# A graph network on one core: the loop over the groups written out, and the light steps at other places among the gate steps

## The reference, cut to what matters

```python
x = _layernorm(x + _L0_gnn_ref(x, adj, W, a_src, a_dst))           # attention, 4 heads: softmax(mask(leaky(...))) @ (x @ W), elu
x = _layernorm(x + _L1_gnn_ref(x, adj, weight, w_ih, w_hh, ...))   # three rounds of: aggregate neighbours, then a GRU cell
x = _layernorm(x + _L2_gnn_ref(x, adj, weight, bias))              # one masked product per relation 1 to 4
x = _layernorm(x + _L3_gnn_ref(x, adj, W, a))                      # attention, 1 head
```

```python
aggr = A.T @ (h @ weight[i])
r = sigmoid(i_r + h_r); z = sigmoid(i_z + h_z); n = tanh(i_n + r * h_n)   # i_* from aggr @ w_ih.T, h_* from h @ w_hh.T
h = (1 - z) * n + z * h
```

## Time and profile before

| what | value |
|---|---|
| median of 3 executions | 3003.52 us (2995.94 to 3004.15) |
| the profiled execution, its own time | 3002.93 us |
| its span, first to last instruction | 3000.9 us |
| mean granted TensorE clock | 0.949 |
| PE busy | 2747.6 us |
| DVE, ACT, POOL busy | 2144.0, 1648.6, 1295.3 us |

### The profile page before, as it was taken

One profiled execution on the slowest core, in us unless ns is written; L12 is line 12 of the kernel. 1 busy time (PEld: TensorE's weight loads), 2 busy tenths in 40 slices (PEclk: granted clock), 3 DMA queues, 4 the chain that ended last, 5 costly groups with the idle time before them and its releaser, 6 DMA issues. The chain is left out here.

```text
span 3000.9 us, 52085 instructions
## 1 busy us (share of the span) xinstructions
PE 2747.6 (92%) x15577; PEld 2353.3 (78%) x15577; DVE 2144.0 (71%) x5170; ACT 1648.6 (55%) x4164; POOL 1295.3 (43%) x1351
## 2 busy tenths in 40 slices
...
DMA packets 97354, 76.18 MB, mean 25 GB/s; under 512 B 6624, under 2 KB 92768, under 8 KB 96992
## 3 DMA queue, kind: packets, MB, share of 16 engines
...
...
## 5 line engine op out<-in xcount | busy, mean ns | idle before, releaser
L943 PE MATMUL psum<-ht_h,whh_h 128*128 128x512 f32 x1152 | 483.5, 420 | 0.0
L943 PE MATMUL psum<-ag_h,wc_h 128*128 128x512 f32 x1152 | 482.4, 419 | 0.0
L943 PE MATMUL psum<-ag_l,wc_h 128*128 128x512 f32 x1152 | 461.6, 401 | 0.0
L943 PE MATMUL psum<-ht_l,whh_h 128*128 128x512 f32 x1152 | 461.4, 401 | 0.0
L943 PE MATMUL psum<-ht_h,whh_l 128*128 128x512 f32 x1152 | 460.1, 399 | 0.0
L943 PE MATMUL psum<-ag_h,wc_l 128*128 128x512 f32 x1152 | 458.4, 398 | 0.0
L1413 POOL TENSOR_TENSOR ht<-ht,g_n 128x512 f32<-128x512 f32 x192 | 256.6, 1336 | 453.9 <-ACT g_n L1104 453.9
L1359 POOL TENSOR_SCALAR rstd<-moments 128x2 f32<-128x2 f32 x256 | 86.6, 338 | 802.1 <-DVE moments L1196 800.6
L943 PEld LDWEIGHTS psum<-ht_h,whh_l 128*128 128x128 f32 x1152 | 220.5, 191 | 54.5
L943 PEld LDWEIGHTS psum<-ag_h,wc_l 128*128 128x128 f32 x1152 | 219.6, 191 | 53.7
L943 PEld LDWEIGHTS psum<-ht_h,whh_h 128*128 128x128 f32 x1152 | 221.8, 193 | 41.6
...
## 6 DMA issues: line engine op xcount, KB each, us to landing
adj_i<-in_adj_dram SPq DMA_DIRECT2D x128, 128.0 KB, 2.1
...
ih_raw<-in_L_gnn_w_ih_dram SPq DMA_DIRECT2D x1, 768.0 KB, 11.9
...
wrs<-in_L_gnn_weight_dram SPq DMA_DIRECT2D x1, 768.0 KB, 11.9
```

What stands on the lines that cost most here:

```text
L943: last = mm(dst, s, m, start=(first and k == 0), stop=(last_part and k == len(flat) - 1))
```

## The change

The loop's segment (groups 2 to 14) becomes 13 segments of one group each, so that all 16 trips are straight code with constants in their waits and addresses. The parts of the program that served the hardware loop go: the second wait in take, the loop in walk, the register forms in after and graphs. TRIP is replaced by another order of the same 254 steps. The order of the gate steps on PE is kept; the light steps, and the shares of gru_n, gru_new, gru_split, gru_turn, gru_turn0, gru_nodes0, gru_keep, gru_norm, gru_load and gru_fin, stand elsewhere. The diff below has the head, some lines of the middle and the tail of TRIP, old and new, and all of the rest.

```diff
 TRIP = """
-last.post_load(0)
-gru_agg(0,0,0)  last.rel_split(0)  next.att_xt(pre,0)
...
-gru_hn(0,0,0)
-gru_rzh(0,0,0)  last.rel_adjt(0)  last.rel_mask(0)  next.att_wh(pre,0,0)  last.gru_fin(1,0)  gru_nodes0(1)
-gru_r(0,0,0)  next.pre_load(0)  last.rel_h1(0)  last.gru_norm(1,0)
-gru_z(0,0,0)  last.gru_fin(1,1)  next.att_wh(pre,0,1)  last.rel_y1(0)  gru_keep(1)
-gru_in(0,0,0)
-gru_hn(0,0,1)  last.rel_rest(0)  gru_load(1)  gru_n(0,0,0)  gru_turn0(1,0)
-gru_rzh(0,0,1)  next.att_scores(pre,0,0)  gru_turn0(1,1)  last.post_load(1)  next.att_scores(pre,0,1)
-gru_r(0,0,1)  last.rel_norm(0)
...
-gru_in(1,1,0)  last.att_res(post,1)  last.rel_rest(2)  gru_turn(0,1,0)
-gru_hn(1,1,1)  gru_turn(0,1,1)  gru_n(1,1,0)  last.att_norm(post,1)
...
-gru_in(1,1,1)  last.att_xt(post,2)
...
-gru_rzh(0,2,1)  gru_split(1,1)  next.att_res(pre,2)  next.pre_load(3)  gru_turn(1,1,0)  last.rel_h1(3)  last.att_pt(post,2,0)
-        gru_turn(1,1,1)  next.gru_load(0)
...
-gru_z(0,2,1)  last.att_pv(post,2)  next.att_wh(pre,3,0)  gru_new(0,2,0)  next.att_norm(pre,2)
-gru_in(0,2,1)  last.rel_y1(3)  last.att_exp(post,2)  last.att_res(post,2)  gru_n(0,2,1)  next.att_wh(pre,3,1)
-        next.att_scores(pre,3,0)  last.rel_rest(3)  next.att_scores(pre,3,1)  gru_new(0,2,1)
-gru_agg(1,2,0)
-gru_agg(1,2,1)  next.att_prob(pre,3)
-gru_hn(1,2,0)  last.att_norm(post,2)
-gru_rzh(1,2,0)  next.att_pt(pre,3,0)  gru_fin(0,0)  next.att_pt(pre,3,1)  next.gru_nodes0(0)  last.rel_norm(3)
-        last.att_store(post,2)
-gru_r(1,2,0)
-gru_z(1,2,0)  last.att_xt(post,3)
-gru_in(1,2,0)  gru_norm(0,0)  gru_fin(0,1)  last.att_wh(post,3,0)  last.att_wh(post,3,1)  next.att_pv(pre,3)
-        last.att_scores(post,3,0)  next.att_exp(pre,3)  last.att_prob(post,3)
-gru_hn(1,2,1)  last.att_pt(post,3,0)  next.att_res(pre,3)  gru_n(1,2,0)  next.gru_keep(0)  next.gru_turn0(0,0)
-        last.att_pv(post,3)  next.gru_turn0(0,1)
-gru_rzh(1,2,1)  next.att_norm(pre,3)  last.att_exp(post,3)
-gru_r(1,2,1)  last.att_res(post,3)
-gru_z(1,2,1)  gru_new(1,2,0)  gru_n(1,2,1)  gru_norm(0,1)
-gru_in(1,2,1)  last.att_norm(post,3)  gru_new(1,2,1)  last.att_store(post,3)
...
+gru_agg(1,1,1)  gru_new(0,1,1)  next.att_exp(pre,1)  gru_split(0,1)
...
+gru_rzh(1,1,0)  last.post_load(3)  last.att_prob(post,1)  last.rel_h1(2)  last.att_pt(post,1,0)
+gru_r(1,1,0)  last.att_pv(post,1)  last.rel_y1(2)  last.att_exp(post,1)  last.att_res(post,1)  next.att_res(pre,1)
...
+gru_in(1,1,1)  next.pre_load(2)  next.att_scores(pre,2,0)
+gru_agg(0,2,0)  gru_n(1,1,1)  next.gru_load(0)
+gru_agg(0,2,1)  next.att_scores(pre,2,1)  last.att_wh(post,2,0)  next.pre_load(3)
+gru_hn(0,2,0)  last.rel_split(3)  next.att_prob(pre,2)
...
+gru_r(0,2,0)  gru_new(1,1,1)  last.att_wh(post,2,1)  next.att_pt(pre,2,0)
...
+gru_rzh(0,2,1)  last.rel_mask(3)  last.att_prob(post,2)  gru_turn(1,1,0)
+gru_r(0,2,1)  next.att_res(pre,2)  last.rel_h1(3)
...
+gru_in(0,2,1)  next.att_wh(pre,3,0)  next.att_norm(pre,2)  last.att_pv(post,2)  gru_n(0,2,1)  gru_turn(1,1,1)  last.rel_y1(3)
+        last.att_exp(post,2)  last.att_res(post,2)  next.att_wh(pre,3,1)  next.att_scores(pre,3,0)
+gru_agg(1,2,0)  last.rel_rest(3)  next.att_scores(pre,3,1)  gru_new(0,2,1)
+gru_agg(1,2,1)
+gru_hn(1,2,0)  last.att_norm(post,2)  next.att_prob(pre,3)
+gru_rzh(1,2,0)  last.rel_norm(3)  next.att_pt(pre,3,0)  gru_fin(0,0)  last.att_store(post,2)
+gru_r(1,2,0)  next.att_pt(pre,3,1)  last.att_xt(post,3)  next.gru_nodes0(0)
+gru_z(1,2,0)  gru_norm(0,0)  gru_fin(0,1)  last.att_wh(post,3,0)  last.att_wh(post,3,1)  last.att_scores(post,3,0)
+        next.att_pv(pre,3)  next.gru_keep(0)  last.att_prob(post,3)  next.att_exp(pre,3)
+gru_in(1,2,0)  next.att_res(pre,3)  last.att_pt(post,3,0)  next.gru_turn0(0,0)  next.gru_turn0(0,1)  gru_n(1,2,0)
+        last.att_pv(post,3)  gru_new(1,2,0)
+gru_hn(1,2,1)
+gru_rzh(1,2,1)  last.att_exp(post,3)  gru_norm(0,1)  last.att_res(post,3)
+gru_r(1,2,1)
+gru_z(1,2,1)  gru_n(1,2,1)
+gru_in(1,2,1)  next.att_norm(pre,3)  last.att_norm(post,3)  last.att_store(post,3)  gru_new(1,2,1)
 """
 
 
@@ -260,9 +257,9 @@
 def make_segments(groups):
     start = [s for s in pre_steps(0) if s] + [("gru_load", 0, (0,))] + flat(between_groups(0, None, 0))
     end = flat(between_groups(1, 0, None)) + [s for s in post_steps(0) if s]
-    return [Segment(start, 0, 1), Segment(trip(True, False), 0, 1), Segment(trip(False, False), 1, 2),
-            Segment(trip(False, False), 2, groups - 1), Segment(trip(False, True), groups - 1, groups),
-            Segment(end, groups - 1, groups)]
+    return [Segment(start, 0, 1), Segment(trip(True, False), 0, 1),
+            *[Segment(trip(False, False), g, g + 1) for g in range(1, groups - 1)],
+            Segment(trip(False, True), groups - 1, groups), Segment(end, groups - 1, groups)]
 
 
 def number_uses(segments):
@@ -661,7 +658,7 @@
 
         def after(eng, semaphore, value):
 
-            if not isinstance(value, int) or value > 0:
+            if value > 0:
                 eng.wait_ge(semaphore, value)
 
         def stand(eng):
@@ -735,12 +732,6 @@
                 tail = earlier[-1]
                 at_end = last_read(resource, Visit(tail.end - 1, tail), tail.takers[resource][k - n])
                 at_end = (at_end[0], at_end[1])
-            if seg.end - seg.first > 1:
-                wrapped = takers[k - n]
-                eng.wait_ge(*last_read(resource, Visit(v.g + -1, seg), wrapped))
-                first = last_read(resource, Visit(seg.first - 1, seg), wrapped)
-                if at_end and first[0] is at_end[0] and first[1] == at_end[1]:
-                    at_end = None
             if at_end:
                 eng.wait_ge(*at_end)
             return k % n
@@ -748,15 +739,9 @@
         def walk(eng, shares):
 
             for seg in segments:
-                if seg.end - seg.first == 1:
-                    for step in seg.order:
-                        if step[0] in shares:
-                            shares[step[0]](Visit(seg.first, seg), step, *step[2])
-                else:
-                    with eng.Fori(seg.first, seg.end) as g:
-                        for step in seg.order:
-                            if step[0] in shares:
-                                shares[step[0]](Visit(g, seg), step, *step[2])
+                for step in seg.order:
+                    if step[0] in shares:
+                        shares[step[0]](Visit(seg.first, seg), step, *step[2])
 
         def slot(v, step, name, args, resource):
 
@@ -770,7 +755,7 @@
         def graphs(v, step, first, n):
 
             at = v.g * 8 + (step[1] * 8 + first)
-            return slice(at, at + n) if isinstance(at, int) else bass.ds(at, n)
+            return slice(at, at + n)
 
 
         @block.sync
```

More of the change, by code:

```diff
@@ L171 @@
-gru_rzh(0,0,1)  next.att_scores(pre,0,0)  gru_turn0(1,1)  last.post_load(1)  next.att_scores(pre,0,1)
-gru_r(0,0,1)  last.rel_norm(0)
-gru_z(0,0,1)
-gru_in(0,0,1)  gru_new(0,0,0)  next.att_prob(pre,0)
-gru_agg(1,0,0)
-gru_agg(1,0,1)  last.att_xt(post,0)  next.att_pt(pre,0,0)  gru_n(0,0,1)  last.gru_norm(1,1)
-gru_hn(1,0,0)
-gru_rzh(1,0,0)  next.att_pt(pre,0,1)
-gru_r(1,0,0)  last.att_wh(post,0,0)  last.rel_split(1)  last.att_wh(post,0,1)  last.rel_adjt(1)  gru_new(0,0,1)
-gru_z(1,0,0)
-gru_in(1,0,0)  last.att_scores(post,0,0)  last.rel_mask(1)  last.att_prob(post,0)  next.pre_load(1)
@@ L182 @@
-gru_hn(1,0,1)  gru_split(0,0)  gru_turn(0,0,0)  next.att_pv(pre,0)  gru_n(1,0,0)
-gru_rzh(1,0,1)  gru_new(1,0,0)  next.att_xt(pre,1)  gru_turn(0,0,1)  last.rel_h1(1)  next.att_exp(pre,0)
-gru_r(1,0,1)  last.att_pt(post,0,0)  next.att_res(pre,0)
-gru_z(1,0,1)  next.att_wh(pre,1,0)
-gru_in(1,0,1)  last.att_pv(post,0)
-gru_agg(0,1,0)  last.rel_y1(1)  last.att_exp(post,0)  last.att_res(post,0)
-gru_agg(0,1,1)  last.rel_rest(1)
-gru_hn(0,1,0)
-gru_rzh(0,1,0)  last.att_norm(post,0)  next.att_norm(pre,0)  next.att_wh(pre,1,1)  gru_n(1,0,1)  last.rel_norm(1)
-        last.att_store(post,0)  next.att_scores(pre,1,0)
@@ L192 @@
-gru_r(0,1,0)  last.post_load(2)
-gru_z(0,1,0)  next.att_scores(pre,1,1)
-gru_in(0,1,0)  last.att_xt(post,1)  next.pre_load(2)  gru_new(1,0,1)  next.att_prob(pre,1)
-gru_hn(0,1,1)
-gru_rzh(0,1,1)  gru_split(1,0)  gru_n(0,1,0)  next.att_pt(pre,1,0)  last.att_wh(post,1,0)  gru_turn(1,0,0)  last.rel_split(2)
-gru_r(0,1,1)  last.att_wh(post,1,1)
-gru_z(0,1,1)  next.att_pt(pre,1,1)  gru_turn(1,0,1)
-gru_in(0,1,1)  gru_new(0,1,0)  last.rel_adjt(2)  last.att_scores(post,1,0)  last.rel_mask(2)
-gru_agg(1,1,0)  next.att_pv(pre,1)  gru_n(0,1,1)  next.att_xt(pre,2)  gru_new(0,1,1)
@@ L238 @@
[L238 to L241 removed]
+gru_hn(0,0,0)  last.rel_split(0)
+gru_rzh(0,0,0)  last.rel_adjt(0)  last.rel_mask(0)  last.gru_fin(1,0)  next.att_wh(pre,0,0)  next.att_wh(pre,0,1)
+        next.att_scores(pre,0,0)
+gru_r(0,0,0)
+gru_z(0,0,0)  gru_nodes0(1)  last.rel_h1(0)
+gru_in(0,0,0)  last.gru_norm(1,0)  next.att_scores(pre,0,1)
@@ new lines @@
```

(9 more changed lines are left out.)

53 lines of the change are left out of this document (35 added, 18 removed).

## The result

The changed kernel takes 2903.43 us (median of 4 runs, 2902.69 to 2904.30); the kernel before took 2999.83 on the same chip (4 runs, 2995.94 to 3004.15). The ratio is 0.9678, 95% interval 0.966 to 0.9697. The forecast was 2908.

What follows compares the result with a forecast made beforehand. PE's own order of work and its waits bound the kernel. Fourteen trips at 166.5 us give 2331, 90 less; with groups 0 and 15, 95 together: 3003 - 95 = 2908 us, range 2872 to 2950.

Steps and rivals of the forecast that it cites:

- Part 1: Loop written out: 69 us less over 14 trips (xt_l wait 24.6, gru_fin wait 11.9, most of 33 from clock).
- Part 2: New order of the steps in TRIP, places changed only: with the straight code, 166.5 us a trip against group 1's 168.0.
- (a): att_scores(pre,3,1), with gru_agg(1,2,0) now between the scores: its 1.3 us wait falls to 0.4, the first's 0.3 to about 0.
- (b): att_pt(post,3,0), now 3.2 us behind its scores: its 1.6 us wait goes, and the 0.2 before att_pv(post,3).
- (c): att_scores(post,3,0), now straight behind att_wh(post,3,1): new wait of 0.6 to 1.3 us, taken as 0.9.
- (d): att_wh(pre,0,0), att_wh(pre,0,1), att_scores(pre,0,0) in a row, over an ACT copy: new wait 0 to 0.4 us, taken as 0.2.
- (e): gru_fin(0,0), the critical one: DVE done at 13.2 us, PE ready at 12.0, new wait 1.3, bounds 0 and 2.4.
- base of 163.4 a trip: Group 1's 168.0 us less its waits of 3.6 and the fill behind five of them, about 0.2 each.
- E: Rival, chance 0.04: no change; the new order makes on DVE what the writing-out saves, 6.5 us a trip.
- covered moves: Rest of the order, including gru_turn(1,1,1), gru_r(1,1,0) and SP and POOL queue moves: counted as hidden behind other work.
- B: Rival, chance 0.24: writing-out gives 69 us, order nothing; DVE-stretched wait stays, clock goes on falling; 2922 to 2958 us.
- D: Rival, chance 0.05, slower: straight code stalls at four skips over absent relations a trip; 176.8 us a trip, 3058 total.

Runs made afterwards that it cites:

- the run without skips: Changed kernel with branch and body of rel_rest's sums over relations 2 and more left out on all four engines: 2905.47 us, ratio 0.9686.

## Why the prediction was right, and where its working was not

The forecast of 2908 was 5 us off, and for the 14 trips it was 2331 against 2329.1. The sum is better than its terms, and that it came so near is in part luck: the clock's 33 us came in full, but not from the part that they were put down to, and other terms cancel.

- **What bounds the kernel**: PE's own order and its waits. It held in every run.
- **Part 1, the waits**: 24.6 and 11.9 us. Right: straight code in the old order saves 27.2 and 11.9, no issue wait of 2 us is left.
- **Part 1, the clock**: wrong. This is the step "most of the 33 us of clock, since group 1 shows none". The straight code with the old order has falls in 13 of 14 trips, and busy time is 4 us more. Part 1 is worth 34 us on these trips instead of 69. What did come is the end of the ten falls behind the back edge; the six falls at the scores became thirteen. Group 1 was a valid sample for the waits and not for the clock: one trip, and the one that holds. The trace of the kernel before could have warned: the same waits at the scores stood in all fourteen trips and cost the clock in six, so they alone don't tell whether it falls.
- **Part 2, the clock**: the other side of it. PE's busy time falls by 38.7 us from old to new order in straight code (2338.9 to 2300.2), and the prediction gave Part 2 nothing of that. Moving gru_agg(1,2,0) between the scores brings 34.7 of it by itself in the old order; taking this step back out of the new order costs only 8, so the rest of the new order keeps the clock in most trips too.
- **(a)** 0.4 forecast, 0.45 measured, and the 0.3 is gone. But this step wins no waiting time, since gru_fin takes it up (in the old order 11.8 us go and 12.3 come; in the new one 1.29 stand against 0.45 and 0.90). Its worth is the clock.
- **(b)** Right: 1.6 and 0.2 gone.
- **(c)** 0.9 forecast, with bounds of 0.6 and 1.3; measured 0.57, just under them.
- **(d)** 0.2 forecast; it is there in one of the fourteen trips, group 3, with 0.18.
- **(e)** 1.3 forecast, 0.90 measured. DVE was done after 13.5 us (forecast 13.2); PE wanted to start at 12.6 and not 12.0. The prediction's own terms (11.7 + 1.8 - 1.6 + 0.4) give 12.3 for PE, and so a wait of 0.9.
- **The base of 163.4 a trip** was too low. It took 1.0 us off for "the fill behind five of them". PE is busy for 164.3 us in each trip of the changed kernel, as it was in group 1 before. This 0.9 and the waits that came out smaller (2.0 to 2.2 instead of 3.0) cancel.
- **Group 0** gave 4.8 for a forecast of 3, since a fall at its scores went too, which the forecast left out. Group 15 gave 2.2 and the end behind it 0.5, for 1 or 2.
- **E's 6.5 us a trip** is what both parts together were to save; the writing-out by itself was put at 69/14 = 4.9.
- **The covered moves** (SP's and POOL's queues, gru_turn) are right: no PE wait belongs to them.

Of the rivals, B had the mechanism of the clock: it "goes on falling", and the straight code with the old order does just that. The new order is what ends it, so B's total didn't come. D, stalls in straight code, is refuted by the trips of 166.2 to 166.6 us and by the run without skips.

What stays open: why group 1, with the same waits in the same straight code, keeps its clock, and why 1.29 us alone (new order) costs it in 3 trips of 14, and 0.30 with 1.29 (old order) in 13 with straight code and in 6 with the loop. The orders also differ in what stands elsewhere in the trip, and no run varies that alone. That the waits at the scores are what the falls hang on is shown for the old order, by one step moved; that they are enough for a fall is not, and these cases speak against it.

None of the six edits of the new order beat it. Between att_pv(post,2) and gru_fin(0,0), and on to att_pt(pre,3,1) and att_xt(post,3), DVE has next to no gap, and in three reorderings there the waits came back elsewhere at the same length or longer. That no order can do better isn't shown.
